# GpSimd's rounding step moved behind two other steps in a hand-written slot order (attention and fp8 linear layer, one core)

## The reference, cut to what matters

```python
# x: (16, 512, 256) float32, 16 heads of 16
x = x + attention(layernorm(x))            # qkv projection, softmax(q k^T / 4) v, output projection
h = layernorm(x)
h_q = clip(h / input_scale, -448, 448).astype(float8_e4m3fn).astype(float32) * input_scale
x = x + h_q @ (weight_fp8 * weight_scale).T + bias
```

## Time and profile before

| | us |
|---|---|
| median of the runs (1001.38 to 1004.5) | 1001.61 |
| time of the profiled execution | 1001.61 |
| its span | 999.2 |
| busy in it: TensorE matmuls | 929.2 |
| VectorE | 847.7 |
| ScalarE | 657.6 |
| GpSimd | 523.8 |

### The profile page before, as it was taken

The page is one execution under the profiler, slowest core; times in us unless marked ns, Lnnn a source line. Parts: engine busy times, 40 slices in busy tenths (PEclk is TensorE's granted clock), DMA queues, the critical chain, the costliest instruction groups (busy, mean ns, idle before and its releaser), DMA issues.

```text
span 999.2 us, 16767 instructions
## 1 busy us (share of the span) xinstructions
PE 929.2 (93%) x5828; PEld 444.6 (44%) x5828; DVE 847.7 (85%) x1250; ACT 657.6 (66%) x1209; POOL 523.8 (52%) x533
## 2 busy tenths in 40 slices
PE   4799999999999999999999999999999999998974
PEld 3453344444444454444444444444444444433323
DVE  3688889898989899898989989898998989889735
ACT  2147777666767767766777766766776766666750
POOL 3332437557382846647384764738385563715162
PEclk9779999999999999999999999999999999999995
DMA  4972635436254555625355653625555362541010
GB/s 149 135 110 39 101 52 106 86 73 111 51 103 73 85 86 87 107 55 104 58 96 76 107 87 64 111 48 105 78 91 87 53 112 34 101 47 44 2 43 21
DMA packets 46452, 79.42 MB, mean 79 GB/s; under 512 B 10144, under 2 KB 13344, under 8 KB 46368
## 3 DMA queue, kind: packets, MB, share of 16 engines
q1 hardware_dynamic: 46368, 78.36, 45.9%
HBM read 18.42 MB, written 8.39 MB: 27 GB/s over the span
## 4 chain that ended last, share of the span: by engine, by line
PE 59%; POOL 25%; DVE 6%; issue 5%; ACT 2%; DMA 1%; SPq 1%; POOLq 0%; DVEq 0%; ACTq 0%
PE ps_t L471 18%; PE ps_o L505 16%; PE ps_s L487 6%; POOL parts L974 5%; PE ps_m L421 5%; PE ps_m L397 5%; PE ps_m L385 3%; POOL hq L1016 3%; POOL hn L1012 3%; POOL h L1006 3%; POOL hn L996 3%; POOL parts L972 2%; PE ps_m L453 2%; DVE mx L717 2%; POOL oT_p L958 2%
## 5 line engine op out<-in xcount | busy, mean ns | idle before, releaser
L595 ACT ACTIVATE pt<-ps_t 128x512 f32<-128x512 f32 x1024 | 558.0, 598 | 222.3 <-PE ps_t L471 218.9
L717 DVE TENSOR_REDUCE mx<-ps_s 128x2 f32<-128x1024 f32 x512 | 613.2, 1209 | 46.8 <-PE ps_s L487 43.6
L471 PE MATMUL ps_t<-qs,ks 50*128 50x512 f32 x1024 | 394.4, 454 | 11.2 <-ACT pt L595 11.0
L487 PE MATMUL ps_s<-ks,qs 48*128 48x512 f32 x1024 | 374.8, 459 | 4.5 <-DVE mx L717 2.7
L471 PEld LDWEIGHTS ps_t<-qs,ks 50*128 50x128 f32 x1024 | 164.8, 185 | 295.9 <-ACT pt L595 203.1
L505 PE MATMUL ps_o<-pt,vt 128*32 128x512 f32 x2048 | 272.5, 604 | 0.0
L983 POOL TENSOR_TENSOR on<-ot,rden 128x256 f32<-128x256 f32 x63 | 39.1, 621 | 241.1 <-DVE rden L778 241.1
L487 PEld LDWEIGHTS ps_s<-ks,qs 48*128 48x128 f32 x1024 | 155.5, 186 | 15.8 <-issue 7.5
L385 PE MATMUL ps_m<-xnT_p,wqkv_p 128*128 128x512 f32 x360 | 104.8, 420 | 1.0 <-POOL xnT_p L952 1.0
L974 POOL TENSOR_TENSOR parts<-parts 128x512 f32<-128x512 f32 x60 | 80.8, 1347 | 4.9
L505 PEld LDWEIGHTS ps_o<-pt,vt 128*32 128x32 f32 x2048 | 40.4, 108 | 86.5 <-issue 86.0
(11 more groups left out here) (94 smaller groups left out, 798.5 us busy)
## 6 DMA issues: line engine op xcount, KB each, us to landing
qs<-parts SPq DMA_DIRECT2D x192, 128.0 KB, 4.5
ks<-parts SPq DMA_DIRECT2D x192, 128.0 KB, 5.3
xin<-in_x SPq DMA_DIRECT2D x16, 512.0 KB, 3.6
xres<-in_x SPq DMA_DIRECT2D x16, 512.0 KB, 4.3
out<-h SPq DMA_DIRECT2D x32, 256.0 KB, 2.0
qs<-nmax SPq DMA_DIRECT2D x256, 4.0 KB
pt<-in_qkv_wT SPq DMA_DIRECT2D x1, 768.0 KB, 5.7
pt<-in_proj_wT SPq DMA_DIRECT2D x1, 256.0 KB, 5.7
```

Of the source, the lines that this page charges most:

```text
L471: nc.tensor.matmul(ps_t[:, g, :], ks[par][rows, slot, keys], qs[par][rows, slot, :], start=True, stop=True).then_inc(st_done, 1)
L487: done = nc.tensor.matmul(ps_s[:, s % 2, g, :], qs[par][rows, slot, queries], ks[par][rows, slot, :], start=True, stop=True)
L595: nc.scalar.activation(pt[n % 2][:, w % 2 + 2 * a, w // 2, :], ps_t[:, a, :], ACT.Exp, scale=SCALE).then_inc(exp_done, 1)
L717: dve.tensor_reduce(mx[:, r, :, s % QUARTER], ps_s[:, s % 2, :, :], AX_X, ALU.max).then_inc(max_done, 1)
```

## The change

In GpSimd's slot, `round_fp8(u - 3)` is called after `split(u, 2)` and `out_divide(u - 2, 2)` instead of ahead of them. The calls themselves, and the other engines' lists, stay as they are.

```diff
                 if present(0) and u > 0:
                     split(u, 1)
-                if present(3):
-                    round_fp8(u - 3)
-                if present(0) and u > 0:
                     split(u, 2)
                 if present(2):
                     out_divide(u - 2, 2)
+                if present(3):
+                    round_fp8(u - 3)
                 if present(0) and u > 0:
                     split(u, 3)
```

## The result

| | us |
|---|---|
| before, median of 4 runs (1001.38 to 1009.37) | 1003.06 |
| after, median of 4 runs (1067.17 to 1070.72) | 1069.2 |
| ratio, with its 95% interval | 1.0646 (1.0594 to 1.0697) |
| span of the profiled execution, after (before: 999.2) | 1067.7 |
| forecast, with its range | 1050 (1029 to 1063) |

The changed kernel is 6.5% slower. The direction was as forecast, and the size was not: the time lies above the range.

The account below looks back on a forecast made before the run. TensorE, busy 93% of the span, was taken as the bound, so its stops were priced. 1001.6 + 27.3 (slots 3 to 15) + 6.8 (slots 16, 17) + 15 (clock) = 1050.7, given as 1050 us, range 1029 to 1063.

Parts of the forecast that it names:

- The chain of causes: GpSimd's divide waits for `rden`, the rounded data comes late, and TensorE stops 3.4 us at L436 instead of at L453.
- the old stop: TensorE's L453 waits for L814, which waits for GpSimd's L1006; 1.18 us a slot, forecast to disappear in slots 3 to 15.
- the 6.8 us of the forecast: Slots 16 and 17: TensorE stops 3.7 and 3.1 us at L436, with no old stop given back.
- `reload` and the stores: SyncE's queue: `reload` is issued 4.1 us later, the stores behind it wait for L814 anyway; cost nothing.
- 3.4 us of stop and 2.1 net: Slots 3 to 15, TensorE at L436: 3.4 less 1.2 and 0.1 given back, 27.3 us over 13 slots.
- the forecast's own best case: Slots 3 to 15: no collision, a stop of 3.05 us, 0.3 us caught up; 1.6 us a slot, 20.8 in all.
- The collision of the third split with L806: VectorE's L806 beside GpSimd's third split grows by 0.31 us, so `rden` comes 0.31 us later; bounds 0 and 0.6.
- the clock term: After the new stops TensorE's clock falls to half in 10 of 15 slots, 3.4 us each: 15 us.
- its upper end of 45 us: A fall in every slot, as long as at the end: 15 x 6.9 x 0.44 = 45 us, total 1081; chance 0.06.
- The rival with the clock kept: The stop alone, with TensorE's clock not falling: 1001.6 + 34 = 1036 us, bounds 1029 to 1042; chance 0.27.
- The sum: Whole kernel: 1001.6 + 27.3 + 6.8 + 15 = 1050.7 us, given as 1050.

Follow-up runs that it names:

- the run with ten fillers: The changed kernel with ten 128x512 matmuls, their result overwritten, on TensorE ahead of its wait for the rounded data in every slot: median 1029.8 us, ratio 1.0221.
- The run with five fillers: The changed kernel with five such overwritten matmuls instead of ten ahead of TensorE's wait in every slot: 1041.6 us in its one run.
- the first group: First group of follow-up runs, with the unchanged kernel run again on that group's chip: median 1008.8 us for that kernel.

## Why the prediction was wrong

**What was right.** The chain of causes and its places. The third split starts at once and costs nothing. The divide waits for `rden` and the rounding behind it comes late, in all 15 slots. TensorE stops at L436 and not at L453, the old stop is given back in 13 slots, and L814 does not wait for L1006. Slots 16 and 17 stop for the 6.8 us of the forecast in the run with the new order there alone. In the changed kernel's own trace it is 3.73 and 1.33 us, since TensorE was at half clock ahead of the second of them and came to it later. `reload` and the stores cost nothing that shows: with the clock kept up, no more is lost than the stop explains.

**The stop, a little too large.** I had 3.4 us of stop and 2.1 net. It is 3.04, and 1.55 net by the run with ten fillers: 13 x 1.55 = 20 us instead of 27.3. That is the forecast's own best case (no collision, 3.05 and 1.6 us). The collision of the third split with L806 came, but it went the other way. I had let VectorE's L806 grow to 1.0 us, and with it `rden` come 0.31 us later. In the slot shown L806 started at 593.62, took its 0.68 us, and GpSimd's L972, which started 0.03 us later, took 1.12 us instead of 0.61. It is the same in all 13 slots with a split. GpSimd had 1.9 us to spare there, so it cost nothing; it only shortened the wait for `rden` to 1.43 us. This is what the Trainium skill, page "SBUF — State Buffer", section "SBUF: two separate sides", says of the shared pair of ports: it goes to the one that starts first, for the whole instruction, and the other waits. The trace agrees on who waits, with 1.12 against 0.61 us; the 0.51 us lost are somewhat less than the 0.65 for which L806 still ran. I had weighed how long the loser waits and not asked who the loser would be, though my own times put L806 (507.34) ahead of the end of the split before (507.42).

**The step that failed: the clock term.** It was "10 of the 15 slots, each 3.4 us at half clock", 15 us, and its upper end of 45 us was given 0.06. There was a fall at each of the 14 stops ahead of slot 17, 6.8 us long at twelve of them, and in slot 17 the clock was low before the stop. By the slots it costs 2.56 us at each of the twelve stops of slots 4 to 15, and 60.1 - 58.88 = 1.2 us at that of slot 3, together 32 us. The ratios go the same way: with the clock kept up by the filler 1.0221, without it 1.0646, so 0.0425 x 1003 = 43 us (34 to 51 by the two intervals) for the clock over the whole kernel, the tail included. The loss for each microsecond at half clock, 2.56 / 6.8 = 0.38, is near the 0.44 taken from the earlier trace rows; the count and the length were at fault. I had halved the only length that a row of a stop gave (6.9 us), with the argument that the work behind the stop is denser than at the end. It was denser (6.33 us busy of 6.80, against 5.49 of 6.90), and the fall was as long. The row should have stood.

I had also read that stop too short. The 2.3 us of the earlier trace rows are a stretch inside it; TensorE stood for 3.71 us there, as the trace of the kernel before shows:

```profile
975.86 1.01 PE L421 MATMUL ps_s<-wproj_p,oT_p 128*128 128x256 f32 x3 [3.71 <-DVE oT_p L880]
```

So the new stop of 3.4 us did not lie above the one with a fall, but between it and the old stops of 1.2 us. The clock fell 2.6 us into that stop (at 974.8), which still speaks for falls, but less firmly than the forecast had it, and no row said what a stop between the two does. The run with five fillers showed falls from 1.6 us on. The rival with the clock kept leaned on 15 harmless stops, where the trace has 13, and its upper bound of 1042 is 1001.6 + 32.5 + 6.8 = 1041.

**The sum again**, with measured terms: 20 for the stops of slots 3 to 15, 32 for their clock, 10 for slots 16 and 17, together 62 of 66 us. In single traces the thin slot 17 adds to the spread. Its stretch at half clock was 27.3 us in the changed kernel's trace, but also 30.7 in that of the run with only the split moved, where nothing had stopped TensorE for over 1.1 us. It is not to be put down to the change alone: the kernel before, in its runs of the first group, went from 1004.6 us at a mean clock of 0.976 to 1015.5 us at 0.956.

## What to carry to other kernels

A step moved in an engine's list takes over the waits of what it is moved behind; look at when that operand is written (here 1.9 us after the split's end), not at how long the steps are. When the move makes a nearly full TensorE stop for longer than it did, read from the trace what its clock did at the longest stop that it shows, the stop taken whole, take that row's length as it is, and multiply by the number of stops; then test it with cheap matmuls in the gap. And a short stop at the end of another engine's list can often be had back by exchanging two independent calls in it, as here for 1.8%.

## What the runs showed of the hardware that was not expected

The clock's loss can be larger than the stop's own (2.56 against 1.55 us a slot), and 150 useless matmuls can make a kernel faster, 1069.2 to 1029.8 us. The Trainium skill, page "TensorE: Matmul & The Clock Gate", section "HAM oscillation — how this bites in real kernels", describes falls that recur in every round of a loop, there at waits between bursts of matmuls. The traces agree, with a fall at each of the 58 stops of 3.0 us and more in five kernels, here between stretches in which TensorE is nearly full. With 1.6 us of the stop empty, 6 of 13 had one; with 1.0 to 1.4 us none had, 13 times in the kernel before and 13 times with only the split moved. Slots with and without falls can settle at a common mean, 61.4 us, in which 0.75 us of added work vanished.
